# Graph layer with sorted edges: message rows stored and gathered as three bf16 parts

## The reference, cut to what matters

```
def mlp(h):
    return relu(h @ w1 + b1) @ w2 + b2
row, col = src, dst                     # 50000 edges, dst sorted
msgs = mlp(xn[col])                     # 50000 x 256
agg  = segment_sum(msgs, row, 3125)     # added up by src
x = x + mlp(xn + agg) + mix(xn)         # mix: an attention of 8 heads over all nodes
x = x + ffn(layernorm(x))               # 16 experts, the 2 best of each node
```

## Time and profile before

| | us |
|---|---|
| median of 3 timed runs | 1455.02 (1454.37 to 1455.14) |
| the profiled execution | 1459.07 |
| its span, first to last instruction | 1457.4 |
| mean granted clock of TensorE, share of full | 0.899 |
| TensorE busy | 1178.5 (81%) |
| VectorE busy | 877.4 (60%) |
| GpSimd busy | 871.9 (60%) |
| ScalarE busy | 536.4 (37%) |

### The profile page before, as it was taken

How to read it: one execution, slowest core, us unless ns; L and a number is a source line. 1 busy time by engine, 2 the same in 40 slices (tenths; PEclk the granted TensorE clock), 3 DMA queues, 4 the chain that set the end, 5 groups by cost and what they waited for, 6 DMA issues and landing times.

```text
span 1457.4 us, 24715 instructions
## 1 busy us (share of the span) xinstructions
PE 1178.5 (81%) x6818; PEld 829.2 (57%) x6819; DVE 877.4 (60%) x2097; ACT 536.4 (37%) x1433; POOL 871.9 (60%) x979
## 2 busy tenths in 40 slices
PE   6799969998737767877877787787896599999966
PEld 4575534433324445544544454454686599999954
DVE  7599979999925555555555555455445544433415
ACT  3567656767402222222322322222343032333224
POOL 5262239999876666666677666665001267765537
PEclk9899989999967998888898899789997599999988
DMA  5000000000032232232232222325386122222266
GB/s 157 16 28 15 15 12 1 0 0 0 15 101 84 87 91 84 87 91 88 87 90 87 87 88 86 90 88 79 117 264 229 30 72 69 71 72 70 69 178 193
DMA packets 50241, 116.01 MB, mean 80 GB/s; under 512 B 11113, under 2 KB 24783, under 8 KB 50040
## 3 DMA queue, kind: packets, MB, share of 16 engines
q0 software_dynamic: 26832, 74.54, 17.7%
q1 hardware_dynamic: 23336, 40.64, 9.2%
HBM read 97.15 MB, written 17.99 MB: 79 GB/s over the span
## 4 chain that ended last, share of the span: by engine, by line
PE 52%; issue 15%; DVE 10%; another core or an unknown queue 7%; POOL 4%; DMA 4%; DVEq 3%; ACT 2%; SPq 1%; POOLq 0%; ACTq 0%
PE bank L1847 13%; PE bank L2098 8%; PE bank L2109 8%; POOL big L678 3%; DVE node_buf L1312 2%; PE bank L1907 2%; PE bank L1791 2%; PE bank L1899 2%; DVE big L1239 2%; PE bank L2011 2%; PE bank L1808 2%; DMA big<-moe_rows 2%; PE bank L1919 1%; PE bank L1717 1%
## 5 line engine op out<-in xcount | busy, mean ns | idle before, releaser
L738 POOL DMA_INDIRECT big<-msg_rows,const x416 | 426.5, 1025 | 193.2 <-issue 95.3
L1312 DVE TENSOR_TENSOR node_buf<-node_buf,bank 125x256 f32 x416 | 174.6, 420 | 290.6 <-PE bank L1847 121.9
L1847 PE MATMUL bank<-big 128*128 128x256 f32 x832 | 266.8, 451 | 63.5 <-DVE node_buf L1312 53.4
L1847 PEld LDWEIGHTS bank<-big 128*128 128x128 f32 x832 | 167.8, 221 | 122.6 <-DVE node_buf L1312 69.7
L994 ACT ACTIVATE big<-bank 128x500 f32<-128x500 f32 (+1 forms) x208 | 110.1, 571 | 240.2 <-remote 122.8
L1239 DVE TENSOR_SCALAR big<-bank,big 125x416 bf16<-125x416 f16 x400 | 180.8, 480 | 0.0
L722 POOL TENSOR_TENSOR big<-big 125x512 f32<-125x512 f32 x125 | 142.2, 1173 | 10.6 <-PE bank L1791 9.3
L1088 ACT ACTIVATE mid<-bank,const 128x128 f32<-128x128 f32 x256 | 73.0, 368 | 194.8 <-PE bank L2098 181.8
L678 POOL TENSOR_TENSOR big<-big 125x256 f32<-125x256 f32 (+1 forms) x100 | 55.4, 554 | 112.6 <-ACT big L815 106.7
L2109 PE MATMUL bank<-big,mid 128*128 x512 | 121.0, 380 | 0.0
L1717 PE MATMUL bank<-big 125*128 125x416 bf16 x400 | 101.9, 345 | 22.0 <-DVE big L1239 11.3
(11 more groups left out here) (317 smaller groups left out, 2103.8 us busy)
## 6 DMA issues: line engine op xcount, KB each, us to landing
big<-L_ffn_w SPq DMA_DIRECT2D x32, 512.0 KB, 6.0
big<-msg_rows,const POOLq DMA_INDIRECT x416
big<-moe_rows SPq DMA_DIRECT2D x10, 560.0 KB
msg_rows<-big SPq DMA_DIRECT2D x25, 125.0 KB
xn_rows<-mid POOLq DMA_DIRECT2D x5, 625.0 KB, 5.9
x_buf<-x SPq DMA_DIRECT2D x5, 560.0 KB
big<-xn_rows SPq DMA_DIRECT2D x5, 560.0 KB
out<-big SPq DMA_DIRECT2D x5, 560.0 KB
```

The source lines that it names most:

```text
L738: pool.indirect_dma_start(msgs[slot], None, msg_rows, bass.IndirectOffsetOnAxis(edge_idx[:, n:n + 1], 0)).then_inc(msgs_in[slot // 2], 16)
L1312: dve.tensor_tensor(rows, rows, agg_ps[2 * half + j][0:P, :], ALU.add).then_inc(s.agg_add, 1)
L1847: mm(agg_ps[k % 4], hot_src[:, turn, k, :], msgs[slot], start=True, stop=True, skip_group_check=True).then_inc(s.agg_mm, 1)
```

## The change

The message rows are stored as three bf16 parts whose sum is the f32 row: `high` is the row rounded to bf16, `middle` the rest rounded to bf16, `low` what is left. A stored row has 3 x 256 bf16 values, 1536 bytes in place of 1024.

In the front, ACT writes `high` from PSUM by one more copy, and then the f32 row. POOL makes the other two parts by a subtraction, a cast and a subtraction (`split`), and releases the store; the loops of SP and POOL over the tiles are written out. POOL does `split(t)` before `halve(t - 1)`. `m_rows` and `m_parts` have two places. In the aggregation a gather brings 1536 bytes per edge, `hot_src` is bf16, and a slot is three bf16 products with the same `hot_src`, added up in PSUM. POOL waits for `v_row_ok` before the first gather, since the slots now reach further.

```diff
-        m_rows = b.take([G, D], parts=P)
+        m_rows = b.take([2, D], parts=P)
+        m_rest = b.take([D], parts=P)
+        m_parts = b.take([2, 3, D], BF16, parts=P)
...
-        msgs = [big[:, 3 * D * k + D:3 * D * k + 2 * D] for k in range(SETS * GB)]
+        msgs = [big[:, 3 * D * k + D:3 * D * k + D + 3 * D // 2].bitcast(BF16) for k in range(SETS * GB)]
...
-        msg_rows = nc.dram_tensor("msg_rows", (N, D), F32).ap()
+        msg_rows = nc.dram_tensor("msg_rows", (N, 3 * D), BF16).ap()
...
-            with sp.Fori(0, T // G) as g:
-                for j in range(G):
-                    sp.wait_ge(s.m_evac, g * G + j + 1)
-                    sp.dma_start(tiled(msg_rows)[:, bass.ds(g * G + j, 1), :].rearrange("p a c -> p (a c)"),
-                                 m_rows[:, j, :]).then_inc(m_out[j], 16)
+            for t in range(T):
+                sp.wait_ge(s.m_parts_ok, t + 1)
+                sp.dma_start(tiled(msg_rows)[:, t, :], m_parts[:, t % 2, :, :].rearrange("p a c -> p (a c)")).then_inc(m_out[t % 2], 16)
...
+            def split(t):
+                high, middle, low = [m_parts[:, t % 2, k, :] for k in range(3)]
+                pool.wait_ge(s.m_evac, t + 1)
+                chain.add(pool.tensor_tensor(m_rest, m_rows[:, t % 2, :], high, ALU.subtract))
+                chain.wait()
+                chain.add(pool.tensor_copy(middle, m_rest))
+                chain.wait()
+                pool.tensor_tensor(low, m_rest, middle, ALU.subtract).then_inc(s.m_parts_ok, 1)
+                pool.wait_ge(s.m_parts_ok, t + 1)
+
+            for t in range(T):
+                split(t)
+                if t:
+                    halve(t - 1)
             halve(T - 1)
...
+            pool.wait_ge(s.v_row_ok, T)
             for n in range(NQ):
...
-                    if not at(g, (0,)):
-                        act.wait_ge(m_out[j], g * 16)
-                    act.activation(m_rows[:, j, :], bank[4][0:P, 0:D], ACT.Copy).then_inc(s.m_evac, 1)
+                    if t >= 2:
+                        act.wait_ge(s.m_parts_ok, t - 1)
+                        act.wait_ge(m_out[t % 2], 16 * (t // 2))
+                    act.activation(m_parts[:, t % 2, 0, :], bank[4][0:P, 0:D], ACT.Copy)
+                    act.activation(m_rows[:, t % 2, :], bank[4][0:P, 0:D], ACT.Copy).then_inc(s.m_evac, 1)
...
-                    mm(agg_ps[k % 4], hot_src[:, turn, k, :], msgs[slot], start=True, stop=True,
-                       skip_group_check=True).then_inc(s.agg_mm, 1)
+                    for part in range(3):
+                        last = mm(agg_ps[k % 4], hot_src[:, turn, k, :], msgs[slot][:, D * part:D * part + D], start=part == 0,
+                                  stop=part == 2, skip_group_check=True)
+                    last.then_inc(s.agg_mm, 1)
```

More of the change, by code:

```diff
@@ L126, in __init__ @@
         self.m_evac = sem("m_evac")
+        self.m_parts_ok = sem("m_parts_ok")
         self.bias_split = sem("bias_split")
@@ L427, in program @@
         b = Region(big, phase, sort_end)
-        msgs = [big[:, 3 * D * k + D:3 * D * k + 2 * D] for k in range(SETS * GB)]
-        hot_src = big[:, 0:SETS * GB * 3 * D].rearrange("p (a k c) -> p a k c", a=SETS, k=GB)[:, :, :, 2 * D:2 * D + 128]
+        msgs = [big[:, 3 * D * k + D:3 * D * k + D + 3 * D // 2].bitcast(BF16) for k in range(SETS * GB)]
+        half_words = big[:, 0:SETS * GB * 3 * D].bitcast(BF16).rearrange("p (a k c) -> p a k c", a=SETS, k=GB)
+        hot_src = half_words[:, :, :, 5 * D:5 * D + 128]
         kv = b.take([2, 4, 128])
@@ L491, in program @@
         s = Semaphores(sem)
-        m_out = [sem(f"m_out{j}") for j in range(G)]
+        m_out = [sem(f"m_out{j}") for j in range(2)]
         msgs_in = [sem(f"msgs_in{k}") for k in range(SETS * GB // 2)]
@@ L679, in halve @@
                     chain.wait()
-                pool.tensor_tensor(norm[:, bass.ds(t, 1), :].rearrange("p a h -> p (a h)").unsqueeze(2),
+                pool.tensor_tensor(norm[:, t, :].unsqueeze(2),
                                    part[:, :, 0:1], part[:, :, 1:2], ALU.add).then_inc(s.norm_part, 1)
[L683 to L693, removed]
+            def split(t):
[11 more added lines that the diff above has]
+                    halve(t - 1)
             halve(T - 1)
-            for j in range(G):
-                pool.wait_ge(m_out[j], 16 * (T // G))
+            for j in range(2):
+                pool.wait_ge(m_out[j], 16 * ((T + 1 - j) // 2))
             chain.add(pool.memset(k_v_rows[:, :, :, 256:257], 1.0))
```

## The result

The changed kernel takes 1471.59 us (median of 4, 1469.11 to 1473.52), the kernel before 1455.08 us beside it on the same chip. The ratio is 1.0103, 95% interval 1.0077 to 1.0129: slower by 1%, clear of noise. The forecast was 1431 us. The profiled execution took 1473.52 us, its span 1471.8 us, 14.4 us more than before, at a mean granted clock of 0.885 (0.899 before).

The account below looks back on a forecast made before the run. In the aggregation PE was taken as the slower partner, with POOL right behind. Front +16 and stage -40 gave -24 us, forecast 1431 us for the median (1455.02 before); own range 1415 to 1446, 8 in 10 1405 to 1470.

Parts of the forecast that it names:

- Of the 189 us on the chain a quarter goes: -47 us: Aggregation: three bf16 products per slot shorten the edge product to 0.75; after 7 us charged, the stage gains 40 us.
- the slower partner, by 67 us: Aggregation: POOL's floor is 551 us, the stage takes 618; the missing 67 us are POOL's waits for PE.
- as unchanged: Chain pieces belonging to no record, such as 18.04 and 4.89 us, were assumed to stay the same.
- the place of PE is taken at once by the adds of DVE: Aggregation, lower end of the gain: DVE's edge adds set the pace instead, and the stage loses nothing.
- The front, +16: Front: extra ACT copy and POOL split per tile cost 5 + 8.5 + 2.4 us; ends +8 and +25.
- The start, +5: Front's start: two splits of 2.1 us before POOL's first halving and ACT's extra copy in three tiles, +5 us.
- A place is reused two tiles later, 10 us or more: hidden: Front: larger stores with two places in place of five were to cost nothing.
- The tail, +2.4: Front's end: the last split goes before the last two halvings, +2.1 us, and 0.3 for the copy.
- The gather, hidden: Aggregation: gathers of 192 KB in place of 128 keep taking POOL 1.025 us, so no change.
- rival A: Aggregation: 1536-byte rows cost POOL more time, so the gather becomes the bound; 1469 us at 15%; chance 0.14.
- C: Front is free because ACT's slack lets POOL lag: only +5 to +7, time 1421 us; chance 0.10.
- rival B: Aggregation: PE's gain does not reach the end; stage gives back 5 to 20 us, 1458 us; chance 0.22.

Follow-up runs that it names:

- chips B: Three chips of the follow-up runs on which the kernel before, unchanged, takes 1455 to 1462 us.
- chips A: Two chips of the follow-up runs on which the kernel before, unchanged, takes 1365 to 1367 us.
- half_gathers_b: Changed kernel with 208 gathers in place of 416, each pair of slots summed from its even slot's rows: 1274.51 us, ratio 0.876.
- before_b: The kernel before, unchanged, run again for its trace: 1457.96 us (one run).
- one_product_b: Changed kernel with one bf16 product a slot in place of three, where the kernel before takes 1455 to 1462 us: 1460.76 us, ratio 1.0035.
- six_products: Changed kernel with each of the three products of a slot taken twice: 1395.64 us, ratio 1.0229.
- after_again: The changed kernel, unchanged, where the kernel before takes 1365 to 1367 us: 1385.32 us, ratio 1.0147.
- one_product: Changed kernel with one bf16 product a slot in place of three, where the kernel before takes 1365 to 1367 us: 1394.24 us, ratio 1.0209.
- slot_hots: Kernel before with its hot matrix made by eight single-slot comparisons in place of one of 128x1024: 1467.79 us, ratio 1.0051.

## Why the prediction was wrong

The step of the prediction that failed is "Of the 189 us on the chain a quarter goes: -47 us", and with it the reading of the earlier trace rows that PE was "the slower partner, by 67 us". The measured term is -2 us, from 638.3 to 636.0 us of stage. The chain was right that the product stood on it. It does not say what comes next when the product is shorter. The waits of POOL for a slot showed that PE was late, not that PE's work made it late. In the same rows DVE waited 106.8 us for a releaser that no record names, and pieces like those of the earlier trace rows made 109 us of the stage's chain. I took them "as unchanged". They grew to 155 us, two thirds of what the product gave up, and "issue" and DVE's adds took nearly all the rest. The runs on chips B show what the stage goes by: leaving out two of the three products takes 11 us off it, leaving out half the gathers 186. What it is in a gather that holds PE's partners up there stays open. On chips A the same term fails in another way: there POOL is at its own floor, and PE's freed time goes into its wait for rows.

The lower end of this term, "the place of PE is taken at once by the adds of DVE", is a second bound, hidden behind the first: the chain of half_gathers_b points to it, where 9 of 49 us are gained.

The other terms:
- The front, +16, measured +14.0. Its steps came out closely: the row copy of the fifth tile is 5.8 us late (+5 was said), the first sort column is multiplied at 125.27 in place of 111.79 us (13.5 late, as said). A split takes 1.98 us where DVE leaves POOL alone (2.1 was said), and between 85.66 and 98.65 us a pair of splits with their halvings takes 12.99 us, 6.5 a tile, as forecast. POOL is busy 39.64 of 52 us in the window from 60 us, and not "nearly full"; up to 73 it still waits for ACT, behind that it is as full as said.
- The start, +5. The size was right (the row copies on ACT that stood at 54.38 and 66.12 us stand at 60.16 and 72.51), the reason only in part. "A place is reused two tiles later, 10 us or more: hidden" is wrong in the first tiles, which come 5 us apart: ACT waits 4.72 us for the store of the first tile, which SP can issue only behind the first split, at 37.28 us.
- The tail, +2.4, measured +1.4: the last row copy on ACT is 12.6 us late (206.77 and 219.40 us), the first key tile 14.0. The last two halvings (221.85 and 225.04 us) are late by the same 14 us against the earlier trace rows.
- The gather, hidden: 1022 ns in place of 1025. A row half as long again costs POOL nothing, and rival A falls. So does C (the front is not free).
- Other small signs came out as said: six product records in 0.83 us, the gather's mean at 1.02. One did not: POOL's waits for a slot fell by 10 us and not to half. And the stage is above 600 us with gathers as before, the sign given for rival B.

B is what happened: the gain did not reach the end, the unnamed pieces took most of its place, and the clock in the stage fell from 0.84 to 0.82. Its price was set too low, at 1451 to 1466 us, because I left it 5 to 20 us of gain where there were 2. The Trainium skill, page "TensorE: Matmul & The Clock Gate", section "HAM oscillation — how this bites in real kernels", was cited for the idle gaps that bring the low clock; the traces agree in direction: in these runs the stage with less work for PE is granted the lower clock. On chips B it is 0.86 with the float32 product (before_b), 0.82 with three bf16 products (the recorded trace) and 0.69 with one (one_product_b); on chips A it is 0.98 with six (six_products), 0.91 with three (after_again) and 0.69 with one (one_product). The page "SBUF — State Buffer", section "Who interferes with whom", held in the front (a split of 1.98 us alone takes 2.56 to 3.30 us beside DVE) and in the stage (slot_hots: gathers of 0.962 us in the mean, against 1.030 in before_b, once DVE's instruction with two inputs is gone). On gathers the section is not of one mind: it also reports that a `tensor_tensor` did not stall the making of descriptors. Here the gathers beside L1294, a `tensor_tensor`, do take longer.

## What to carry to other kernels

An item's share of the chain is an upper bound for what shortening it may bring, and a poor estimate where two or three partners stand close behind each other: ask for each of them what the stage would take if it were alone. Pieces of the chain that no record explains can be a bound like any other; a term that rests on the stage's slack has to say why these would let go. And a change that relieves one engine by loading another in an earlier stage pays its cost in any case and earns only if the relieved engine sets the pace. Here leaving out work of the suspected engine altogether (one product in place of three) would have told it in one run.

## What the runs showed of the hardware

- The same program takes 1366 us on two chips and 1455 to 1462 us on three others and in the recorded pair, on each of them within 1%. The whole difference lies in the stage with 416 indirect gathers (545 against 637 us); what stands before and behind it takes the same within 3 us. With 208 gathers the changed kernel takes 1270.5 us on a chip A and 1274.5 on a B.
- An indirect gather of 128 rows holds POOL 0.945 us (median) and 0.305 us before the next, whether a row has 256, 1024 or 1536 bytes.
- A gather that starts beside a DVE instruction of 128x1024 with two inputs in SBUF can take 1.77 us; the 32 gathers of the kernel before that take over 1.5 us all start so. Beside eight instructions of 128x128 with one input and a scalar column none takes over 1.5 us (slot_hots).
